# Wide attention: values of two pairs in every second tick, v-projections in ticks 1, 3, 5 and 7

## What is computed

```python
# layer 0
q, k, v = jnp.split(jnp.einsum('btc,oc->bto', x, wqkv), 3, axis=-1)   # 16 heads of 64
q, k = _rope(_rmsnorm(q, q_norm_w), cos, sin), _rope(_rmsnorm(k, k_norm_w), cos, sin)
attn = jnp.einsum('bhtd,bhsd->bhts', q, k) * scale
attn = jax.nn.softmax(jnp.where(causal, attn, -jnp.inf), axis=-1)
out = jnp.einsum('bhts,bhsd->bhtd', attn, v)
return jnp.einsum('bte,ce->btc', out, wo)
# layer 1
scores = jnp.einsum('bhqd,bhkd->bhqk', q, k) * scale + bias
attn = jax.nn.softmax(scores, axis=-1)
return jnp.einsum('bhqk,bhkd->bhqd', attn, v) @ o_w.T
```

## Time and profile before

| | us |
|---|---|
| median of 3 runs | 2936.32 (2935.26 to 2938.88) |
| the profiled execution | 2937.82 |
| its span, first to last instruction | 2936.0 |
| wide attention of layer 0 in the span | about 67 to 656 |
| wide attention of layer 1 in the span | about 1047 to 1644 |
| mean granted TensorE clock | 0.982 of full speed |

### The profile page before, as it was taken

The page is one execution under the profiler, slowest core; times in us unless marked ns, Lnnn a source line. Parts: engine busy times, 40 slices in busy tenths (PEclk is TensorE's granted clock), DMA queues, the critical chain, the costliest instruction groups (busy, mean ns, idle before and its releaser), DMA issues.

```text
span 2936.0 us, 68986 instructions
## 1 busy us (share of the span) xinstructions
PE 2779.8 (95%) x25484; PEld 1870.2 (64%) x25484; DVE 2121.7 (72%) x5801; ACT 1699.2 (58%) x4109; POOL 1042.3 (36%) x1422
## 2 busy tenths in 40 slices
PE   5999999989999999999999799999989998999898
PEld 2666666666666666666666455477767765666676
DVE  6988888855666566666666599855668885887775
ACT  3888888873333377777676477644325544343665
POOL 6888888831000011111111345312243330104441
PEclk9999999999999999999999899999989999999999
DMA  3011111122000011111111555300035443244760
GB/s 106 22 25 31 31 31 31 30 77 99 7 9 1 1 35 31 31 31 31 31 30 22 147 148 137 96 1 16 1 107 146 125 120 77 59 102 119 200 180 27
DMA packets 191998, 186.98 MB, mean 64 GB/s; under 512 B 14529, under 2 KB 168193, under 8 KB 190897
## 3 DMA queue, kind: packets, MB, share of 16 engines
q1 hardware_dynamic: 191664, 182.56, 24.3%
HBM read 129.19 MB, written 53.31 MB: 62 GB/s over the span
## 4 chain that ended last, share of the span: by engine, by line
PE 76%; DVE 10%; ACT 6%; issue 3%; SPq 2%; POOL 2%; DMA 1%; DVEq 0%; ACTq 0%; POOLq 0%
PE pb L161 68%; ACT big L947 4%; PE pb L643 3%; ACT big L158 2%; DVE big L2188 2%; DVE big L817 2%; PE pb L576 1%; SPq L1869 1%; PE pb L2159 1%; DVE big L233 1%; PE pb L246 1%; DVE big L2679 1%; DMA big<-parts 1%; DVE big L727 1%; DVE big L800 0%
## 5 line engine op out<-in xcount | busy, mean ns | idle before, releaser
L161 PE MATMUL pb<-big 64*128 64x256 bf16 (+12 forms) x20300 | 2520.7, 330 | 97.7 <-DVE big L2188 36.4
L161 PEld LDWEIGHTS pb<-big 128*128 128x128 f32 (+5 forms) x20300 | 1569.5, 145 | 847.3 <-issue 504.0
L158 ACT ACTIVATE big<-pb 128x512 f32<-128x512 f32 (+7 forms) x1444 | 828.2, 623 | 549.9 <-PE pb L161 309.6
L158 ACT ACTIVATE big<-pb,big 128x512 f32<-128x512 f32 (+2 forms) x536 | 315.5, 616 | 545.0 <-PE pb L161 481.1
L2188 DVE TENSOR_REDUCE big<-pb 128x4 f32<-128x1024 f32 (+1 forms) x256 | 278.4, 1087 | 84.1 <-PE pb L161 79.5
L172 POOL TENSOR_TENSOR big<-big 128x128 f32<-128x128 f32 x192 | 84.8, 456 | 653.5 <-DVE big L169 653.5
L947 ACT ACTIVATE big<-big 128x256 f32<-128x256 f32 x512 | 253.9, 498 | 69.1 <-DVE big L822 68.1
L947 ACT ACTIVATE big<-pb,big 128x128 f32<-128x128 f32 (+1 forms) x512 | 256.7, 526 | 61.8 <-DVE big L802 61.6
L817 DVE CUSTOM_DVE_ANT_0 big<-pb,big 128x256 f32<-128x256 f32 x512 | 186.6, 421 | 99.2 <-PE pb L161 99.2
L1543 DVE SCALAR_TENSOR_TENSOR big<-pb,big 128x128 f32<-128x128 f32 x512 | 144.1, 344 | 138.1 <-PE pb L161 137.3
L1026 POOL TENSOR_TENSOR big<-big 128x512 f32<-128x512 f32 x128 | 159.7, 1275 | 232.1 <-DMA big<-recip 232.0
(11 more groups left out here) (147 smaller groups left out, 2192.8 us busy)
## 6 DMA issues: line engine op xcount, KB each, us to landing
big<-parts SPq DMA_DIRECT2D x96, 512.0 KB, 4.2
parts<-big SPq DMA_DIRECT2D x384, 96.0 KB, 2.4
big<-recip SPq DMA_DIRECT2D x64, 512.0 KB, 6.8
big<-comb SPq DMA_DIRECT2D x32, 512.0 KB, 8.2
parts<-big SPq DMA_DIRECT2D x192, 64.0 KB, 2.1
big<-gates SPq DMA_DIRECT2D x7, 1024.0 KB, 6.1
big<-in_wf SPq DMA_DIRECT2D x1, 3072.0 KB, 14.8
big<-scratch SPq DMA_DIRECT2D x1, 3072.0 KB, 17.6
```

Of the source, the lines that this page charges most:

```text
L158: return e.activation(o, i, f, bias=bias, scale=scale)
L161: return e.matmul(o, l, r_, start=start, stop=stop, skip_group_check=True)
```

## The change

The values of two pairs follow one another in every odd tick from t = 3 (value(t - 3), value(t - 2)). For this TS becomes a ring of three; the third lies on WM in layer 0, and on the end of WF and WM in layer 1, so the loads of CT and WM for the next modulation are issued later, in the narrow attention of layer 1. The quarters of the v-projection move from u = 2, 3, 4, 5 to u = 3, 5, 7 and, for the last, to u = 1 of the batch's own ticks; the first value of a batch waits for it, no longer the first scores. The transpose of the reciprocals goes from u = 1 to 2, scale0 and scale1 from 3 and 4 to 4 and 5, the norm's transposes and modulation from u = 0 to 2. In gpsimd_tick the scalings come first. In layer 1 the row maxima of the first head are negated and signalled before those of the second are taken, and the exponentials run head by head. The stage has one tick more. The diff, cut to its core:

```diff
-            TS = [alloc(2 * width) for _ in range(2)]
+            TS = [alloc(2 * width) for _ in range(2)] + [WM if causal else big[:, spare_at:spare_at + 1024]]
...
-            last = 128 + 2
+            last = 128 + 3
...
-            v_at = (2, 3, 4, 5)
+            def values_in(b, u):
+                found = (b - 1, 3) if u == 1 else (b, u // 2 - 1) if u in (3, 5, 7) else None
+                return [found] if found and 0 <= found[0] < 16 else []
...
-                return [(step, t // 8 - 1) for step, late in (("recip", 0), ("turn", 1), ("scale0", 3), ("scale1", 4), ("c0", 6), ("c1", 7))
+                return [(step, t // 8 - 1) for step, late in (("recip", 0), ("turn", 2), ("scale0", 4), ("scale1", 5), ("c0", 6), ("c1", 7))
...
-                return (a + 1) // 2 if a < 15 and a % 2 == 1 and u == 0 else None
+                return (a + 1) // 2 if a < 15 and a % 2 == 1 and u == 2 else None
...
-                if 0 <= b < 16 and u in v_at:
-                    take("v", b, v_at.index(u), ring=ring)
+                for v in values_in(b, u):
+                    take("v", *v, ring=ring)
...
                 b, j, c = p // 8, p % 8, p // 2
+                if j == 0:
+                    for n in (2, 3):
+                        s = slots["v", b, n]
+                        e.wait_ge(s.free, s.n)
...
-                    if 0 <= t - 2 < 128:
+                    if t >= 3 and t % 2:
+                        value(e, t - 3)
                         value(e, t - 2)
...
-                                                   nm[:, 2 * qt + i:2 * qt + i + 1])
-                t.then_inc(own_v.sem, own_v.up())
-                e.wait_ge(own_v.sem, own_v.n)
-                e.tensor_scalar(nm, nm, -1.0, None, ALU.mult).then_inc(pair_maxed, 1)
+                                                   nm[:, 2 * i + qt:2 * i + qt + 1])
+                    t.then_inc(own_v.sem, own_v.up())
+                    e.wait_ge(own_v.sem, own_v.n)
+                    e.tensor_scalar(nm[:, 2 * i:2 * i + 2], nm[:, 2 * i:2 * i + 2], -1.0, None, ALU.mult).then_inc(pair_maxed, 1)
...
-                if p >= 2:
-                    e.wait_ge(pair_valued, p0 + p - 1)
+                if p >= 3:
+                    e.wait_ge(pair_valued, p0 + p - 2)
...
             def gpsimd_tick(e, t, a, b, u):
+                for step, c in posts(t):
+                    if step in ("scale0", "scale1"):
+                        half = int(step[5])
+                        e.wait_ge(ld_recip, 32 * (b0 + c + 1))
+                        for i in (2 * half, 2 * half + 1):
+                            k = 4 * c + i
+                            e.wait_ge(chunk_out, c0 + k + 1)
+                            e.tensor_tensor(OT[k % 6], OT[k % 6], R[:, 2 * i:2 * i + 2, :], ALU.mult).then_inc(chunk_scaled, 1)
...
-            left = (3, 4, 6, 7)
+            left = (4, 5, 6, 7)
...
                     if k == 1 and b == 5:
                         tail.sync(e)
+                        e.dma_start(CT, dr["c2"]).then_inc(ld_wm, 16)
+                        e.dma_start(WM, dr["wmod2"]).then_inc(ld_wm, 16)
```

More of the change, by code:

```diff
@@ L113, in program @@
         WF = alloc(6400)
+        spare_at = top[0] - 256
         WM = alloc(768)
@@ L586, in tensor_extra @@
             def tensor_extra(e, t, a, b, u):
-                if 0 <= b < 16 and u in v_at:
-                    tensor_v(e, b, v_at.index(u))
+                for v in values_in(b, u):
+                    tensor_v(e, *v)
                 for step, c in posts(t):
@@ L611, in scores @@
                 if j == 0:
-                    for key in (("v", b, 2), ("v", b, 3)) + ((("turn", b, 7),) if causal else (("project", b, 6), ("project", b, 7))):
+                    for key in (("turn", b, 7),) if causal else (("project", b, 6), ("project", b, 7)):
                         s = slots[key]
@@ L649, in turned_out @@
                 n = width // 64
-                return (TS[p % 2].rearrange("p (n q) -> p n q", n=n)[:, :, 64 * half:64 * half + 64],
+                return (TS[p % 3].rearrange("p (n q) -> p n q", n=n)[:, :, 64 * half:64 * half + 64],
                         banks[2 * (p % 2) + half][:, 0:width].rearrange("p (n q) -> p n q", n=n))
@@ L663, in value @@
                         t = mm(e, o[64 * i:64 * i + 64, 256 * (p % 2) + q0:256 * (p % 2) + 256], VB[b % 2][:, kb, 2 * j + i, :],
[L664 removed]
+                               TS[p % 3][:, width * i + 256 * kb:width * i + 256 * kb + 256 - q0], kb == 0, kb == 1)
                 t.then_inc(pair_valued, 1)
@@ L772, in vector_extra @@
                         residual_vector(e, r0 + qt, qt, bk[:, 0:128], 0).then_inc(s.free, 1)
-                if 0 <= b < 16 and u in v_at[0::2]:
-                    vector_v(e, b, v_at.index(u))
+                for v in values_in(b, u):
+                    if v[1] % 2 == 0:
+                        vector_v(e, *v)
                 c = normed_in(a)
@@ L887, in vector @@
                         guest.vector(e, t - guests_at)
+                e.wait_ge(pair_valued, p0 + 128)
             def scalar_v(e, b, n):
@@ L922, in scalar_extra @@
             def scalar_extra(e, a, b, u):
-                if 0 <= b < 16 and u in v_at[1::2]:
-                    scalar_v(e, b, v_at.index(u))
+                for v in values_in(b, u):
+                    if v[1] % 2:
+                        scalar_v(e, *v)
                 c = turned_in(a, u)
@@ L935, in exps @@
                 s, b, j = p % 2, p // 8, p % 8
-                e.wait_ge(pair_maxed, p0 + p + 1)
+                e.wait_ge(pair_maxed, p0 + (p + 1 if causal else 2 * p + 1))
                 if p >= 2:
@@ L940, in exps @@
                     e.wait_ge(recip_made, b0 + b - 1)
-                for qt in range(2):
+                for n in range(4):
+                    qt, i = (n // 2, n % 2) if causal else (n % 2, n // 2)
                     at = 0 if qt == 0 else width - 256
                     w = 128 if causal and qt == 0 else 256
[L944 to L949, removed]
+                    if n == 2 and not causal:
+                        e.wait_ge(pair_maxed, p0 + 2 * p + 2)
+                    ps, h = PS[s][:, i, at:at + w], 2 * j + i
+                    t = e.activation(ps, banks[2 * s + i][:, at:at + w] if causal else ps, ACT.Exp, bias=NM[s][:, n:n + 1],
+                                     scale=rstd_q(b)[:, qt, h:h + 1] if causal else 1.0,
+                                     accum_out=SM[b % 2][:, 2 * h + qt:2 * h + qt + 1])
                 t.then_inc(pair_exped, 1)
@@ L1019, in gpsimd_tick @@
                 for step, c in posts(t):
-                    if step in ("scale0", "scale1"):
-                        half = int(step[5])
-                        e.wait_ge(ld_recip, 32 * (b0 + c + 1))
-                        for i in (2 * half, 2 * half + 1):
-                            k = 4 * c + i
-                            e.wait_ge(chunk_out, c0 + k + 1)
-                            e.tensor_tensor(OT[k % 6], OT[k % 6], R[:, 2 * i:2 * i + 2, :], ALU.mult).then_inc(chunk_scaled, 1)
-                    elif step in ("c0", "c1"):
+                    if step in ("c0", "c1"):
                         qt = 2 * c + int(step[1])
```

2 lines of the change are left out of this document (removed).

## The result

The changed kernel took 2970.3 us (median of 4, 2968.9 to 2971.5) beside 2935.8 us of the kernel before on the same chip: ratio 1.0113, 95% interval [1.0101, 1.0124]: 33 us slower by the ratio, which is what the experiments below are compared by, 34.5 by the two medians. The forecast was 2968. The profiled execution took 2968.9 us, span 2967.0, against 2937.8 and 2936.0 before.

A forecast was written before the change was run, and what follows sets the result against it. TensorE, busy 98 to 99% of both wide stages, bounds the kernel. Layer 0 +31 us (+2.55 a full batch), layer 1 nothing (-0.05 a batch), stage ends +0.5: 2936.3 becomes 2968 us, range 2942 to 2988.

The forecast's parts named there:

- Point 1: Values of two pairs together: each merged group saves a 0.15 us tile-shape passage, -0.6 us a batch in both layers.
- Point 3: Layer 0, tick 7: output projection c1 waits for the bank of its own tick's projection, +1.96 us.
- Points 4 and 5: Layer 0: norm's transposes in tick 2 wait 1.7 to 1.8 us for a bank; c0 waits 1.8 us for scalings.
- Point 8: Today's waits in ticks 0 and 1 counted as gone: -1.05 us a batch in layer 0, -1.0 in layer 1.
- Point 6: Norm's statistics on VectorE in tick 0 of every second batch: 0.9 us late there, +0.45 a batch.
- Layer 0 together: Sum of layer 0's terms: +2.55 us a batch, 31 us over the stage.
- Point 7: Layer 1, row maxima in halves: an extra 0.20 us negation delays the copy and scores, +1.55 us a batch.
- A: Rival: no new wait comes, only saved passages and old waits count; 45 us less, 2891; chance 0.1.
- B: Rival: only c1's bank binds, reciprocals land sooner and the norm's bank is free; +10 us, 2947; chance 0.12.
- C: Rival: layer 1 gains because the copy isn't last there; 23 us less, 2945; chance 0.1.
- D: Rival: upper bounds, c0 waits 3.1 us and layer 1 at 2.5; up to 2999, likely 2988; chance 0.1.
- E: Rival: B and C at once, the waits half as long; no difference, 2936; chance 0.04.

The follow-up runs named there:

- experiment 1: The changed kernel with one v-projection of layer 0 moved from tick 7 to tick 0, so tick 7 takes three banks: 2944.2 us, 1.0019 of the kernel before.
- experiment 7: The changed kernel with GpSimd's layer 1 scalings cut to 8 of 256 columns, the rest left unscaled: 2956.3 us, 1.0067 of the kernel before.
- experiment 3: The changed kernel with layer 1's row maxima negated once a tick with one signal, as before, not in halves: 2980.7 us, 1.0136 of the kernel before.

## Why the prediction was right, point by point

**Point 1, the pairing's 0.15.** 1.88 us for two pairs in layer 1 where two single ones take 2.04: 0.16 saved. In layer 0 1.46 for 1.62. The passage from turns straight to the projection, which no row of before showed, costs 0.59 (0.46 in layer 0) as the one to the values does. Right.

**Point 3, c1's bank.** 1.96 forecast, 1.96 found, 13 times; with what hangs on it 27 of the 33 us, by experiment 1. This worked because both dates stood in rows of the same tick: ScalarE's end, which hangs on scores that don't move, and TensorE's arrival.

**Points 4 and 5, the norm's bank and the reciprocals.** The norm's wait is 1.78 (1.7 to 1.8 forecast). The chain to the last scaling takes 17.6 us, and c0 starts 17.65 after the transpose (17.9 forecast), but c0 waits 0.41 and not 1.8: TensorE's way was dated too short by 1.1. Most of the missing time is two waits on the way, for a bank that ScalarE holds and for the exponentials:

```profile
550.86 1.13 PE L162 MATMUL pb<-big 128*128 128x512 f32 x2 [0.28 <-ACT big L159]
...
562.77 0.59 PE L649 MATMUL pb<-big 64*128 64x64 f32 x12 [0.50 <-ACT big L963]
```

By the distance of the starts these are 0.36 and 0.67 here, 0.57 and 0.48 in the batch that starts at 146.79. **Point 8** had the waits of today as gone; in layer 0 waits of this kind stayed. The two errors cancel, because c0's date is set by the chain, whatever lies on the way: a batch without the norm is 36.0 + 1.96 + 0.41 + 1.0 = 39.37 long, where I had 36.0 + 1.96 + 1.8 = 39.8. The term was mis-sized, the sum wasn't; that the two terms share one date the prediction didn't say.

**Point 6, the statistics.** 0.9 forecast. The one long period that has no statistics behind it is 40.23, where the five others are 41.05 to 41.57: 0.8 to 1.3. One period is thin evidence.

**Layer 0 together.** 41.2 + 39.4 - 2 x 37.64 = 5.3 us in two batches, 2.65 each; 2.55 forecast. Twelve periods cost 31.1 us; 30.6 forecast. Over the whole stage it is 36.3, where I had 31: the 5 more lie at the stage's two ends. The first turn comes 2 us sooner than before, layer 1 is 3 us shorter, and so the end comes out as forecast; that these make up for the 5 is luck.

**Point 7, layer 1.** Of the waits behind the copy, tick 1 has 0.43 (0.65 forecast), tick 3 0.22 (0.4), tick 5 0.50, or 0.99 with a norm (0.4). 1.15 to 1.6 a batch against 1.55. Right in sum, but tick 5 for a reason that I didn't have: GpSimd's scalings, which the change moved to ticks 4 and 5, hold up the negations that the change had doubled. I had the negation at its 0.2 us from one row, where GpSimd is idle, and never looked at how its length spreads, which the trace of before would have shown (experiment 7). Today's waits of turns did go, as forecast, and the halves did it (experiment 3). Layer 1 ends 3 us shorter, I had it at nothing.

**The rivals.** A, no new wait, and B, only c1's bank, were too low, by the norm's 1.78 and the old waits that stay under c0's chain. B named the largest cause, four fifths of the loss by experiment 1, but set today's waits against it, which stayed. C, a gain in layer 1, had a little truth, 3 us of 23. D asked for a landing later than 11 us after the transpose; it came at 10.4, at most 10.9. E, no difference, asked for smaller waits in layer 0 and a gain of layer 1 at once; the first didn't come.

## What to carry to other kernels

A ring of buffers binds as soon as one step takes more of it than it has: count the takes of each step before and after a move, and date the release of the one that comes round from rows that don't move. Work that is bunched in every second step saves its own passages and gives uneven steps, and the short steps wait for the other engines. A low busy share is no cover: the pairing alone cost more in layer 1, where VectorE and ScalarE were busy 67 and 71% of the time, than in layer 0. The 0.6 us saved a batch were paid with more, until the signals were made to come earlier. A sum of waits that go is half a forecast; ask of each what is late next, and put the halves of a cost on different engines before the whole on another.

## What the runs showed of the hardware

VectorE's negation of two numbers a partition took 0.169 us alone and up to 1.06 beside GpSimd's product of 512, ending within 0.03 us of the end of a GpSimd operation in each of the 28 long cases; these, and what else the cut scalings gave room to, were worth 9 us of layer 1, since each stands ahead of what TensorE waits for. VectorE's product of four numbers a partition in layer 0 (L814) took 0.16 us in the mean of the 42 cases where GpSimd stood still, and 0.31 in the mean of the 86 where it ran beside. For TensorE, a value group that follows another one directly is 0.16 us shorter than one between steps of other shapes, in both layers.
